# A fused vision tower on one core: attention norm and first projections of image 0 set amid the first expert layer, the other images' projections set one pair at a time between the first attention tiles

## What is computed

```python
x  = h + shared(n) + gated_experts(n)          # layer 0, n = norm(h)
n  = layernorm(x)                              # the attention norm
q  = einsum('btd,hrd->bhtr', n, Q)             # 8 heads, r = 32
k  = einsum('bud,hrd->bhur', n, K)
scores = einsum('bhtr,bhur->bhtu', q, k) / sqrt(d)
ctx = einsum('bhtu,bud->bhtd', softmax(scores), n)
out = einsum('bhtd,hde->bte', ctx, VO)
```

## Time and profile before

| | us |
|---|---|
| median of 3 runs | 611.97 |
| lowest, highest | 611.20, 613.12 |
| the profiled execution's own time | 613.25 |
| its span, first to last instruction | 611.4 |
| mean granted TensorE clock | 0.984 of full |

### The profile page before, as it was taken

The page is one execution under the profiler, slowest core; times in us unless marked ns, Lnnn a source line. Parts: engine busy times, 40 slices in busy tenths (PEclk is TensorE's granted clock), DMA queues, the critical chain, the costliest instruction groups (busy, mean ns, idle before and its releaser), DMA issues.

```text
span 611.4 us, 10204 instructions
## 1 busy us (share of the span) xinstructions
PE 563.2 (92%) x3076; PEld 330.1 (54%) x3076; DVE 373.6 (61%) x881; ACT 328.4 (54%) x726; POOL 75.2 (12%) x89
## 2 busy tenths in 40 slices
PE   0689799997989999999999999999999999997994
PEld 0454344443556566566576576666666676452441
DVE  3844754214697667677677577577577677036562
ACT  0464758563746456466466465465465565536521
POOL 0000000000696100100100100100100001112000
PEclk9999999998989999999999999999999999999997
DMA  6500000000551322322322422323323320000015
GB/s 171 227 0 2 0 0 2 0 1 14 125 144 40 102 72 66 99 68 73 93 64 75 97 58 78 94 58 82 90 58 88 84 58 19 2 1 1 1 39 119
DMA packets 21986, 37.65 MB, mean 62 GB/s; under 512 B 5560, under 2 KB 15224, under 8 KB 21704
## 3 DMA queue, kind: packets, MB, share of 16 engines
q1 hardware_dynamic: 21606, 36.82, 23.3%
q10 hardware_dynamic: 354, 0.50, 0.4%
HBM read 6.07 MB, written 2.41 MB: 14 GB/s over the span
## 4 chain that ended last, share of the span: by engine, by line
PE 89%; ACT 4%; DVE 2%; DMA 2%; issue 1%; SPq 0%; DVEq 0%
PE P L702 86%; DMA X<-x 2%; PE P L718 2%; PE P L985 1%; ACT L504 1%; ACT PT L610 1%; ACT g L642 1%; DVE bst L1187 1%; PE P L1125 0%; DVE xhat L1259 0%; SPq L369 0%; ACT act L513 0%; PE P L844 0%; PE P L955 0%; DVE mx L1395 0%
## 5 line engine op out<-in xcount | busy, mean ns | idle before, releaser
L1395 DVE TENSOR_REDUCE mx<-P 112x1 f32<-112x392 f32 x448 | 219.0, 557 | 96.2 <-PE P L702 91.8
L610 ACT ACTIVATE PT<-P 112x392 f32<-112x392 f32 x448 | 188.2, 494 | 26.6 <-PE P L702 25.5
L702 PE MATMUL P<-Ks,Qs 96*112 96x392 f32 x448 | 167.8, 379 | 1.0 <-DVE mx L1395 0.9
L702 PE MATMUL P<-Qs,Ks 98*112 98x392 f32 x448 | 155.3, 351 | 0.8 <-ACT PT L610 0.7
L702 PE MATMUL P<-PT,XVs 112*64 112x392 f32 x896 | 154.5, 496 | 0.0
L702 PEld LDWEIGHTS P<-PT,XVs 112*64 112x64 f32 x896 | 61.6, 137 | 79.3 <-issue 73.6
L702 PEld LDWEIGHTS P<-Ks,Qs 96*112 96x112 f32 x448 | 78.8, 178 | 42.7 <-issue 19.7
L618 ACT ACTIVATE CT<-P 128x392 f32<-128x392 f32 x32 | 15.9, 497 | 134.4 <-PE P L702 134.4
L702 PEld LDWEIGHTS P<-Qs,Ks 98*112 98x112 f32 x448 | 79.9, 179 | 6.2 <-ACT PT L610 3.7
L688 POOL TENSOR_TENSOR OUT<-OUT,part 120x448 f32<-120x448 f32 x27 | 30.7, 1136 | 274.1 <-DVE part L1422 274.1
L702 PE MATMUL P<-VBs,CT 128*112 128x130 f32 (+1 forms) x320 | 40.0, 261 | 0.6 <-ACT CT L618 0.6
(11 more groups left out here) (180 smaller groups left out, 466.3 us busy)
## 6 DMA issues: line engine op xcount, KB each, us to landing
Qs<-QKH SPq DMA_DIRECT2D x64, 98.0 KB, 2.2
Ks<-QKH SPq DMA_DIRECT2D x64, 98.0 KB, 2.2
XVs<-XV SPq DMA_DIRECT2D x32, 196.0 KB, 2.5
Qs<-QKL SPq DMA_DIRECT2D x32, 98.0 KB, 2.1
Ks<-QKL SPq DMA_DIRECT2D x32, 98.0 KB, 2.1
X<-x SPq DMA_DIRECT2D x4, 588.0 KB
wa<-table_a SPq DMA_DIRECT2D x1, 2207.5 KB, 8.3
VBs<-VB SPq DMA_DIRECT2D x32, 65.0 KB, 2.2
```

Of the source, the lines that this page charges most:

```text
L610: nc.scalar.activation(PT[:, u, c * HALF:(c + 1) * HALF], P[0:T, SCORE_BANK + half_in_loop(s, u, c) % RING, 0:HALF], ACT.Exp, scale=float( ...
L702: return nc.tensor.matmul(dst, lhsT, rhs, start=start, stop=stop, **more)
L1395: nc.vector.tensor_reduce(mx[:, s % 2, c, t:t + 1], bank(n)[0:T, :], AX.X, ALU.max)\
```

## The change

- The norm of image 0 leaves the common attention norm. In TensorE's list `centre(0)` stands in the turn of image 1 behind its shared second layer, the variance (`variances((0,), 4)`) behind the gate rows of image 1, `spread_rstd((0,))` in the turn of image 2, `centre(1)` in that of image 3. VectorE copies, squares and multiplies image 0 behind its sums into `H`. ScalarE has its Ln, Exp and two table loads behind the first layer of image 2.
- Pairs (0,0) and (0,1) stand in the turn of image 3, ahead of its third layer, in banks 0 to 3. They alone are split by ScalarE and VectorE.
- Pairs (0,2) and (0,3) stand under the wait for the remaining norm. They are copied raw and split by GpSimd, as are all others: 28 halves (`RAW`).
- Pairs (1,0) to (1,3) go into the lead. `BETWEEN` now has 12 pairs and 3 turns, none behind tile 8.
- SyncE fills the slots of heads 0 and 1 ahead of the values of images 1 to 3; the first waits for queries and keys apart.
- The memory of layer 0's buffers is laid out in another order (with unused pieces), so that queries and keys of image 0 can be written while image 3 is in its third layer.

```diff
+        BETWEEN = {0: (("qk", 1, 0),), 1: (("qk", 1, 1),), 2: (("qk", 1, 2),), 3: (("qk", 1, 3),), 4: (("qk", 2, 0),),
+                   5: (("xv", 1), ("qk", 2, 1)), 6: (("qk", 2, 2),), 7: (("qk", 2, 3),), 9: (("qk", 3, 0),),
+                   10: (("xv", 2), ("qk", 3, 1)), 11: (("qk", 3, 2),), 12: (("qk", 3, 3),), 13: (("xv", 3),)}
+        RAW = [(b, n) for b in range(B) for n in range(4) if b or n >= 2]
...
+                if b == 2:
+                    nc.scalar.preload_act_table_set(LN)
+                    scalar.wait_ge(var_full, ATT + 1)
+                    rstd(rs[0:R, :], P[0:R, 4, 0:HALF], eps[0:R, :])
...
-            for n in range(4):
+            nc.scalar.preload_act_table_set(LN)
+            for n in range(2):
                 project_high(n)
-            for n in range(4):
-                project_raw(1, n)
+            for b in range(1, B):
+                scalar.wait_ge(centred, 4 * (ATT - GATE) + b + 1)
+                nc.scalar.activation(sq[:, b, :], bank(3 + b), ACT.Square).then_inc(squared, 1)
+            scalar.wait_ge(var_full, ATT + 2)
+            rstd(rs[:, :], bank(7), eps[:, :])
+            for n in range(2, 4):
+                project_raw(0, n)
...
+                if b == 2:
+                    spread_rstd((0,), ATT + 1)
+                elif b >= 1:
+                    centre(b // 2)
...
+                if b == B - 1:
+                    for n in range(2):
+                        project_pair(0, n)
                 for m in range(E0):
...
-            norm(ATT, h_ready, lambda b: B + b + 1)
+            centre(2)
+            centre(3)
+            variances(range(B), 7)
+            for n in range(2, 4):
+                project_pair(0, n)
+            spread_rstd(range(1, B), ATT + 2)
```

More of the change, by code:

```diff
@@ L403, in _ @@
             features_in(0)
-            sync.wait_ge(qk_lo, 4)
-            fill_stacks(0, 0)
-            features_in(1)
+            fill_stacks(0, 0, queries=2, keys=4)
             fill_stacks(0, 1)
-            features_in(2)
-            features_in(3)
+            for b in range(1, B):
+                features_in(b)
             for s in range(2, 4):
@@ L489, in _, with rstd @@
             tokens_out(6, 0)
+            def rstd(dst, variance, small):
+                nc.scalar.activation(dst, variance, ACT.Ln, bias=small).then_inc(act_step, steps.one())
+                nc.scalar.preload_act_table_set(EXP)
+                scalar.wait_ge(act_step, steps.now())
+                nc.scalar.activation(dst, dst, ACT.Exp, scale=-0.5).then_inc(rstd_ready, 1)
             def norm(S):
@@ L501, in norm @@
                                          **({} if bias_of(S) is None else dict(bias=bias_of(S)))).then_inc(squared, 1)
[L502 to L506, removed]
+                scalar.wait_ge(var_full, round_of(S))
+                rstd(rstd_buf(S)[:, :], bank(var_bank(S)), eps[:, :])
             norm(TOK2)
@@ L883, in broadcast_gate, with project_pair, centre, variances @@
                 mm(bank(WBC_BANKS[n % 2]), sel, rows).then_inc(wbc_full, 1)
+            qk = A("qk").rearrange("p (q g h n) -> p q g h n", q=2, g=2, h=2)
+            def project_pair(b, n):
+                q, g = QK_ORDER[n]
+                for h in range(2):
+                    if (b, n) in RAW:
+                        m = RAW.index((b, n))
+                        banks = raw_banks(m)
+                        if m < 2:
+                            pe.wait_ge(qk_lo, 2 * m + h + 1)
+                        elif m < 4:
+                            pe.wait_ge(normed, 4 * ATT + B)
+                        else:
+                            pe.wait_ge(qk_raw, 2 * (m - 2) + h + 1)
+                    else:
+                        banks = FIRST_RING[n]
+                    rows = slice(h * D, (h + 1) * D)
+                    mm(bank(banks[h]), qk[rows, q, g, h, :], xhat[rows, b, :]).then_inc(qk_full, 1)
+            def centre(b):
+                pe.wait_ge(h_ready, B + b + 1)
+                if b == 1:
+                    pe.wait_ge(normed, 4 * ATT + 1)
+                mm(bank(max(4, 3 + b)), Bt("center"), H[:, b, :]).then_inc(centred, 1)
+            def variances(images, n):
+                for b in images:
+                    pe.wait_ge(squared, B * ATT + b + 1)
+                    if b == 0 and n == 4:
+                        pe.wait_ge(copied, B * (ATT - POOL3) + 1)
+                    last = mm(P[b * R:(b + 1) * R, n, 0:HALF], means[:, :], sq[:, b, :])
+                last.then_inc(var_full, 1)
+            def spread_rstd(images, ready):
+                pe.wait_ge(rstd_ready, ready)
+                for b in images:
+                    pe.wait_ge(copied, B * (ATT - POOL3) + b + 1)
+                    rows = slice(b * R, (b + 1) * R)
+                    mm(bank(max(4, 3 + b)), spread[rows, :], rs[rows, :]).then_inc(rstd_full, 1)
+            def rows_amid(b):
+                rows_of(b)
+                if b == 1:
+                    variances((0,), 4)
             logits(A("gw"), MOE0)
@@ L1048, in four_heads @@
                         context_tile(i, s, u, first and s == 0)
+            turn_values(0)
+            pe.wait_ge(qk_raw, 4)
             for j in range(LEAD):
```

103 lines of the change are left out of this document (49 added, 54 removed).

## The result

The changed kernel took 605.93 us (605.02 to 607.36, 4 runs), the kernel before 611.59 (610.97 to 613.12, 4 runs): a ratio of 0.9899, interval [0.9876, 0.9922], so about 1.0% faster and 0.17 us from the forecast. (The quotient of the two medians is 0.9907, their difference 5.66 us, where the forecast took 5.9 off 611.97.) In later runs it took 606.19 (605.73 to 607.89, 6 runs), 0.9909 [0.9882, 0.9935] of the kernel before. The profiled execution took 607.36, its span is 605.6, the mean granted clock 0.983.

A forecast was written before the change was run, and what follows sets the result against it. TensorE bounds the kernel (89% of the last-ending chain). The lead starts 8.75 us earlier, less its lengthening and a new 0.65 wait: gain 5.9 us, so 611.97 - 5.9 = 606.1, range 603.5 to 608.8.

The forecast's parts named there:

- Added to the experts: TensorE's work for image 0's norm and pairs amid the experts: third layer ends 3.1 us later, at 144.3.
- ScalarE's gap: Idle 4.18 us between hidden copies amid the experts: takes image 0's 3.7 us of Ln, Exp and loads, 0.45 slack.
- the page of the Trainium skill: Says a table switch on ScalarE costs a drain of some 1.38 us besides the load; the gap would overrun by 2.3.
- The wait under the norm: TensorE's wait for the remaining norm's inverse roots, ahead of the spread: 1.0 us against 2.52.
- The lead's lengthening: Lead up to the first maxima's transpose 11.9 us for 11.0, from there to its end 8.4 for 6.4.
- The new wait for the last values: Behind the lead, TensorE waits 0.65 us for ScalarE's copy of the last turned values, on TensorE's path.
- The fall under the norm: Half clock from the attention norm on; sum assumed full clock; rival that it falls as before: 607.6 to 609.3, chance 0.11.
- The fall behind the lead: Half clock in the first head's maxima and scores; rival without it: 1.5 us more gain, 604.6, chance 0.13.
- ended its splits: GpSimd's 28 halves, started at 150.4, end near 193.8, as before; nothing waits for them.
- VectorE's three multiplications beside it: Norm, rival: GpSimd holds each multiplication by 0.8 us, pair (1,0) is 2.4 late; 608.5, chance 0.04.
- the one on the gap's overrun: Rival amid the experts: two table switches overrun ScalarE's gap by 2.1 us, TensorE waits; 608.2, chance 0.04.
- the one on half clock through the lead: Rival: the fall under the norm lasts through the lead, 19.7 us of work doubles; 625.8, chance 0.02 with like stalls.

The follow-up runs named there:

- experiment 5: The changed kernel with one more table load in ScalarE's list ahead of the Ln of image 0: 608.0 us, 0.9922 of the kernel before.
- experiment 6: The changed kernel with image 2's values behind tile 8 and image 3's behind tile 10 instead of 10 and 13: 606.74 us.
- experiment 1: Matmuls that nobody reads, put into TensorE's waits: nine in the changed kernel, 603.44 us; these and three more in the kernel before, 610.23 us.
- experiment 3: The changed kernel with image 1's four pairs back ahead of the lead, behind the turn of image 0's values: 607.47 us, 0.9926 of the kernel before.
- experiments 2 and 3: The changed kernel with image 1's four pairs back ahead of the lead: ahead of turning image 0's values 610.15 us, behind it 607.47 us.
- experiment 4: The changed kernel with image 1's four pairs ahead of the lead and pairs (0,0), (0,1) behind the third layer: 611.16 us.

## Why the prediction was right, step by step

- **Added to the experts: +3.1 forecast, +3.04 measured** at the third layer's end. Its parts: `centre(0)` and the variance together +0.78, by the anchors of image 1's second shared layer and what follows, where I had 1.0; the single spread +0.85 (124.11 to 124.96) where I had 0.65; `centre(1)` +0.25 as forecast, the wait behind it down to 0.58; the two pairs +1.16 for 1.2.
- **ScalarE's gap: hidden, as forecast, but with no slack.** I had 0.45 us over, on the ground that "all of it is shifted alike". It isn't: counted from the fourth spread, the hidden copies ahead of the gap start 1.24 us later (30.41 against 29.17; the variance matmul stands ahead of their matmuls, and ScalarE waits 0.46 for them), the one behind it 0.78 (36.14 against 35.36). So the gap shrank from 4.18 to 3.71 us. The chain ends at the moment the next copy can start, and experiment 5 shows 1.09 of 1.28 us coming through. The load costs 1.28 and no drain appears, so the trace keeps disagreeing with the page of the Trainium skill that the forecast weighed ("ScalarE: Activation LUTs", What ACT_TABLE_LOAD costs).
- **The wait under the norm: 1.0 us forecast, 1.00 measured**, and the lead starts at 152.43 where I had 152.0. Half of the difference is that everything stands 0.21 later from the start of the program.
- **The lead's lengthening was mis-sized.** The step "from 171.77 on, 6.4 us becomes 8.4" counted 8.4; from 164.05 to the end of the last tile, about 171.5, are 7.5; the part ahead of it took 11.6 for 11.9. VectorE's tail and TensorE's pairs fit into each other better than I assumed. From the `XV,wb` matmul to the second transpose the lead grew by 1.4 us; I had 2.9.
- **The new wait for the last values** is there with 0.63 of the forecast 0.65, but it is not on the path, as experiment 6 shows. With it TensorE's path to the second transpose was 1 us shorter than I had it: 173.99 instead of 175.0.
- **The clock: partly luck.** The fall under the norm is gone in my sum without a word: from 147.1 us on it is worked out at full clock, while the rows that it starts from hold that fall, which cost 1.85 us (experiment 1). So about 4.0 of my 5.9 us were the moved work, which measured 5.2. (I also read both falls as 6.4 us long; by the earlier trace rows they last 6.8.) The fall behind the lead I let be the same, and counted a gain for the case without it. In this profile that case came true (another 1.0 us by the third transpose), and a fall in the last norm took 2.15 back. I had not thought of falls outside the seam, nor of the half rate at the start. The sum, 5.9 us, came out partly by luck: 1.2 too little at the seam and the 1.0 behind it stand against the 2.15 lost in the last norm.
- **GpSimd** ended its splits at 194.0, forecast 193.8, and nothing waited for it. VectorE's three multiplications beside it took 1.51 us, 0.5 each: that rival falls. So do the one on the gap's overrun and the one on half clock through the lead. The clock behind the lead stayed up in this profile and fell in the second, at 173, so that rival is open.

Where the gain comes from, at full clock and by anchors: of the 5.2 us, about 2.0 are the four pairs in the lead (experiment 3), 1.5 the wait for the norm of images 1 to 3 that turning and the first tile now cover (experiments 2 and 3), 0.4 the pairs ahead of the third layer (experiment 4). The remaining 1.3 are the norm of image 0 amid the experts with its pairs under the shorter wait; I have no kernel that shows this part alone at full clock. The shares go by the order in which the parts were taken back: the kernel before has no wait of 1.68 us, so the 1.5 are what the new order would have lost without that cover.

## What to carry to other kernels

Where one engine paces a stretch, put its work where it would wait for another, one small piece at a time, and look at what the moved work itself waits for: the four pairs ahead of the lead cost 2.5 us by the norm they waited for and the fall that followed, and 2.0 by their own work (experiments 2 and 3). Before two profiles are compared, compare their granted clock slice by slice, compare the durations of like matmuls too (at the start the clock's row read 1.00 at half rate), and measure between anchors; a difference in a stretch that nobody touched is a warning that the totals mix two things. And on a kernel bound by TensorE, matmuls that nobody reads, put into its longest waits, can be worth nearly as much as the change under study; here, by the anchors, the two at the start were worth most.

## What I had not expected

Idle time of TensorE can cost twice. A wait of 0.66 us (experiment 5) was followed by 3.4 us at 1.2 GHz and 1.4 us of loss on top of the 1.09; falls followed waits in all parts of the program, at other places in each profile, and the same wait of 2.52 us in the last norm had a fall behind it in one profile and none in another (the earlier trace rows against 547 after). Eleven matmuls of 0.7 us each, whose results are never used, took 4.9 us off the median of the changed kernel (606.19 to 601.26), nearly as much as the change itself, and 3.1 of the 5.0 us between the two profiles were won ahead of the second norm's spread, where the clock's row reads 1.00 in both. What exactly sets the moment of a fall stays open; no run here shows it.
